# An attention-and-FFN layer on one core: a reordered prologue that issues from two queues

## Chip, core and metric

The kernel runs on one core of a Trainium2 chip. The metric is device time in microseconds, from one launch to its end; the median of three runs is compared.

## What is computed

Eight batches of 512 tokens with 128 channels pass an attention layer with 16 heads of 8 channels, a layer norm, a gated feed-forward layer and a second layer norm. The scores of a head are a sum of three things: a tanh of the scaled q.k product, a product of "soft bits" (hamming) and a "lattice" form of six features per token. The part that the change touches is the making of q, k and the features, and the constants behind them:

```python
qkv = (x @ qkv_w.T).reshape(b, t, 3, H, HD)
scores = sips_alpha[0] * jnp.tanh(raw / sips_beta[0])
soft_bits = jnp.tanh(x @ hex_w.T)
hamming = jnp.einsum('bid,bjd->bij', soft_bits, soft_bits) / 2.0
scores = scores + lam * hamming[:, None, :, :]
hexc = jnp.tanh(x @ q6_w.T)
w = jax.nn.softmax(transform_weights / TEMP, axis=-1)
Mh = jnp.einsum('ht,tde->hde', w, transforms)
lat = jnp.einsum('bid,hde,bje->bhij', hexc, Mh, hexc) / 6.0
attn = jax.nn.softmax(scores + lat * (jax.nn.sigmoid(scale_logit) * 2.0), axis=-1)   # causal
x = layernorm(x + out); r = sigmoid(xr @ W_r.T); k = relu(xk @ W_k.T) ** 2
x = layernorm(x + r * (k @ W_v.T))                                  # xr, xk mix x with the token before
```

## The kernel before, in words

Each batch has a period of 20 steps (`PAIRS`), numbered t. A step handles one "pair", a 128 x 1024 block of scores in one of three PSUM buffers (`raw`). For a pair TensorE makes q.k (`scores`), ScalarE takes the tanh (line 783), TensorE makes the bias (`biases`: lattice, hamming and a shift, one step later) in the same buffer, VectorE adds the two (`main`, line 1004), ScalarE takes the exponential three steps later (line 788), GpSimd masks it (line 892), and TensorE multiplies by v into `sums` (`weighted`). The buffer is free for pair t + 3 when `main` of pair t has run, so the engines go in a ring of three. Five pairs make a quad of four heads; quad 1 begins at t = 5.

q, k, J (the features as keys) and G (the features as queries, with the lattice matrices applied) are split into three bf16 levels each: `hi` is a rounding cast, `rest` the difference, `mid` a second cast, `lo` the last difference. They go to DRAM (`to_dram`) and come back replicated as stacks (`load_stack`), from which bf16 matmuls make the products at full precision. Everything in a batch's side work that passes through the one `side_bank` of PSUM is a "unit": xT (transposed x), q, k, F (features), G, v. Units have a fixed order; TensorE starts a unit when the reader of the one before has finished. A period makes units xT2, q2, k2, F2, G2 for two batches ahead and v1 for one batch ahead.

Engines execute in order, so the order in the code is the order of the work. Before the first period there is a prologue that is written out by hand:

- SyncE issues every load but those of x (line 352 on): x of batch 0, the q/k/v weights, the feature weights, then seven small constants (lines 359 to 363), the late weights (out_w, W_r, W_k, W_v, lines 366 to 370). `first_stacks` (line 447) then writes and loads q and k for the first four heads, J, G, the shift rows (line 465), heads 4 to 8, and heads 8 to 16, and writes the rows of batch 1.
- VectorE (line 1147 on) copies the weights, makes batch 0's q, k, J, G levels with GpSimd's help (`rest`, `lo`, lines 950 to 952), makes the lattice matrices, the bound that gives the shift (lines 1215 to 1226), the values of batch 0 (`values_in(0)`), then the late weights (lines 1231 to 1247), and then batch 1's units from `x_out(1)` on (line 1250).
- TensorE (line 689 on) runs units xT1, q1, k1, F1, the small lattice products, G1, v1, the scores of pair 0, then four late transposes (line 714), batch 1's xT2, q2, k2, F2, the scores of pair 1, G2, and enters period 0. There it runs batch 2's xT2 and then the bias of pair 0.

Of the kernel before, what the change touches and what calls it, by code (L numbers as in the profile page):

```python
# [25 lines left out]
ACT = mybir.ActivationFunctionType  # L26
# [6 lines left out]
DVE0_BETA = 6  # L33
DVE0_WEIGHTS = 10
DVE0_TWMAX = 12
# [4 lines left out]
DVE0_SHIFT = 30  # L40
DVE0_END = 37
# [31 lines left out]
ACT_UNITS = {"F1", "F2", "kk", "rr"}  # L73
FIRST_UNITS = ["xT1", "q1", "k1", "F1", "G1", "v1", "xT2", "q2", "k2", "F2", "G2"]
# [8 lines left out]
def period_uses(post, prep, values):  # L83

    return [use for t in range(PAIRS) for use in units_at(t, post, prep, values)]


class Side:
# [26 lines left out]
    def made(self, n, use):  # L115

        if use == "v" or isinstance(n, int) and n == 0:
            return self.through(n - 1, use + "1")
        return self.through(n - 2, use + "2")
# [20 lines left out]
def build(nc, x, qkv_w, out_w, hex_w, lam_logit, q6_w, transforms, transform_weights, scale_logit,  # L140
# [17 lines left out]
    with ExitStack() as ctx:  # L158
# [118 lines left out]
        x_in = sem("x_in")  # L277
# [7 lines left out]
        first_qk, first_g, second_in = sem("first_qk_in"), sem("first_g_in"), sem("second_in")  # L285
# [29 lines left out]
        def side_place(b, use):  # L315

            if use in ("q1", "k1"):
# [31 lines left out]

        @block.sync  # L350
        def _(sp):
# [24 lines left out]
            def to_dram(kind, par):  # L376

                done = scr_in[kind]
                if kind == Q:
                    sp.dma_start(q_rows[par].rearrange("l p i -> p l i"), parts[:, Q]).then_inc(done, 16)  # L380
                elif kind == K:

                    sp.dma_start(k_rows[par][0:LEVELS].rearrange("l p i -> p l i"), parts[:, K]).then_inc(done, 16)
                    sp.dma_start(k_rows[par][LEVELS:].rearrange("l p i -> p l i"),
                                 parts[:, K, 0:LEVELS - 1]).then_inc(done, 16)
                elif kind == J:
                    sp.dma_start(j_rows[par], parts[0:J_ROWS, J]).then_inc(done, 16)
                else:
# [971 lines left out]
```

## Time and profile before

| | us |
|---|---|
| median of three runs | 420.8 (420.11 to 423.27) |
| the profiled execution | 420.74 |
| its span, first to last instruction | 418.8 |
| busy: TensorE matmul, VectorE, ScalarE, GpSimd | 368.2, 332.7, 327.3, 230.6 |
| prologue: start of the first `main` | 47.53 |

The profile's busy shares are averages over the span: the prologue (the first 45 us) and the tail are sparse, the periods between them dense. What an instruction costs is read from its own row. The profiled execution's time is 1.9 us above its span.

### The profile page before, as it was taken

The page shows a single profiled execution, that of the slowest core. Times are in us where ns is not written, and L with a number is a line of the kernel's source. Part 1 is how long each engine was busy: PE and PEld are TensorE (multiplying, and loading weights), DVE is VectorE, ACT ScalarE, POOL GpSimd, SP SyncE. Part 2 cuts the span into 40 slices and gives each one's busy share as a digit, 9 for nine tenths or more (in the row PEclk, how much of TensorE's full clock was granted, in tenths as well). Part 3 has the DMA queues.
Part 4 walks back from the last instruction along what each step waited for, and adds up shares of the span by engine and source line. Part 5 has one row for each costly group of instructions (what it writes and reads, how often), then busy time and mean ns, then how long its engine had stood idle before and what let it go on. Part 6 is the DMA issues. An engine that isn't in the chain of part 4 may idle for free.

```text
span 418.8 us, 8760 instructions
## 1 busy us (share of the span) xinstructions
PE 368.2 (88%) x2907; PEld 191.3 (46%) x2907; DVE 332.7 (79%) x539; ACT 327.3 (78%) x364; POOL 230.6 (55%) x367
## 2 busy tenths in 40 slices
PE   4557798899999999999899989999989998999863
PEld 1232343345455544645364535454544554345442
DVE  4873677988988989798979897989887958786643
ACT  1002389999998989799889989899989998999621
POOL 4313535834687359644965488646873446344532
PEclk9999999999999999999999999999999999899978
DMA  3354587786621775167624764276318610100000
GB/s 100 94 144 121 162 275 189 232 236 166 200 84 48 205 193 172 49 164 195 190 80 121 188 182 131 85 194 186 123 52 206 173 59 7 45 27 1 2 27 25
DMA packets 37807, 53.74 MB, mean 128 GB/s; under 512 B 3522, under 2 KB 35266, under 8 KB 36190
## 3 DMA queue, kind: packets, MB, share of 16 engines
q1 hardware_dynamic: 34078, 51.49, 43.4%
q10 hardware_dynamic: 3696, 1.84, 1.8%
q8 instruction: 18, 0.29, 0.3%
q14 instruction: 15, 0.12, 0.1%
HBM read 38.69 MB, written 14.61 MB: 127 GB/s over the span
## 4 chain that ended last, share of the span: by engine, by line
PE 50%; DVE 15%; issue 10%; POOL 9%; SPq 7%; ACT 5%; DMA 3%; ACTq 1%; POOLq 0%; DVEq 0%
PE raw L511 22%; PE side_bank L511 13%; PE sums L511 12%; DVE probs L1004 6%; ACT probs L788 3%; PE side_bank L598 3%; POOL probs L892 2%; SPq L401 2%; ACT probs L783 2%; POOL x L927 2%; POOL x L923 2%; SPq L415 2%; POOL parts L905 2%; SPq L412 2%; DVE bn L1089 1%
## 5 line engine op out<-in xcount | busy, mean ns | idle before, releaser
L1004 DVE SCALAR_TENSOR_TENSOR probs<-probs,scal,raw 128x1024 f32<-128x1024 f32 x160 | 202.8, 1274 | 40.4 <-PE raw L511 39.4
L783 ACT ACTIVATE probs<-raw 128x1024 f32<-128x1024 f32 x160 | 163.9, 1025 | 33.2 <-PE raw L511 32.2
L892 POOL TENSOR_SCALAR_AFFINE_SELECT probs<-probs 128x256 f32<-128x256 f32 (+1 forms) x224 | 98.9, 458 | 131.6 <-ACT probs L788 131.1
L788 ACT ACTIVATE probs<-probs 128x1024 f32<-128x1024 f32 x160 | 169.3, 1060 | 0.9 <-DVE probs L1004 0.9
L511 PE MATMUL raw<-q_stack,k_stack 72*128 72x384 bf16 (+3 forms) x512 | 99.0, 306 | 10.9 <-DVE probs L1004 6.9
L511 PE MATMUL raw<-i_stack,j_stack 111*128 111x384 bf16 (+3 forms) x512 | 98.1, 304 | 2.7 <-ACT probs L783 2.5
L511 PE MATMUL sums<-probs,values 128*32 128x256 f32 (+2 forms) x1280 | 93.3, 391 | 5.1 <-POOL probs L892 4.1
L511 PEld LDWEIGHTS raw<-q_stack,k_stack 72*128 72x128 bf16 x512 | 38.9, 99 | 63.8 <-DVE probs L1004 35.3
L511 PEld LDWEIGHTS raw<-i_stack,j_stack 111*128 111x128 bf16 x512 | 42.4, 99 | 48.6 <-issue 15.3
L511 PEld LDWEIGHTS sums<-probs,values 128*32 128x32 f32 x1280 | 29.8, 109 | 50.9 <-issue 27.2
L899 POOL TENSOR_TENSOR whole<-whole,parts 128x512 f32<-128x512 f32 x22 | 26.2, 1189 | 23.1 <-DVE parts L1038 23.1
L905 POOL TENSOR_TENSOR parts<-whole,parts 128x512 bf16<-128x512 f32 x30 | 35.1, 1171 | 4.2 <-DVE parts L1043 4.2
L1043 DVE CAST parts<-whole 128x512 bf16<-128x512 f32 x32 | 19.6, 612 | 2.9 <-POOL whole L899 2.8
L915 POOL TENSOR_TENSOR rstd<-var_eps,minus_half 128x4 f32<-128x4 f32 x14 | 14.7, 1047 | 1.2
L796 ACT ACTIVATE feats<-side_bank 128x512 f32<-128x512 f32 x8 | 4.9, 611 | 12.4 <-PE side_bank L511 12.4
L511 PEld LDWEIGHTS side_bank<-w_r_mix,x1T 128*128 128x128 f32 x112 | 13.6, 191 | 1.0
L511 PE MATMUL side_bank<-w_r_mix,x1T 128*128 128x128 f32 x112 | 13.6, 275 | 0.0
L511 PE MATMUL side_bank<-x1T,w_k_mix 128*128 128x512 f32 x28 | 13.2, 591 | 0.0
L835 ACT ACTIVATE probs<-shift_col 1x1536 bf16<-1x1536 bf16 x1 | 1.5, 1481 | 14.6 <-DVE w_r_mix L1244 14.6
L1038 DVE CAST parts<-whole 128x512 bf16<-128x512 f32 x24 | 12.3, 511 | 0.7 <-DMA q_rows<-parts 0.5
L1089 DVE BATCH_NORM_STATS2 bn<-res 128x6 f32<-128x128 f32 x56 | 12.2, 280 | 0.2
L511 PE MATMUL side_bank<-xT,wqT 128*128 128x512 f32 x14 | 9.7, 781 | 2.9 <-DVE xT L1019 2.3
(144 smaller groups left out, 347.6 us busy)
## 6 DMA issues: line engine op xcount, KB each, us to landing
q_stack<-q_rows SPq DMA_DIRECT2D x21, 384.0 KB
k_stack<-k_rows SPq DMA_DIRECT2D x21, 384.0 KB
i_stack<-lattice_i SPq DMA_DIRECT2D x21, 288.0 KB
i_stack<-hamming_i SPq DMA_DIRECT2D x21, 288.0 KB
q_rows<-parts SPq DMA_DIRECT2D x8, 384.0 KB, 8.7
k_rows<-parts SPq DMA_DIRECT2D x8, 384.0 KB, 3.0
lattice_i<-parts SPq DMA_DIRECT2D x8, 288.0 KB
k_rows<-parts SPq DMA_DIRECT2D x8, 256.0 KB, 3.3
```

The costliest lines, as they stand in the source:

```text
L511: return nc.tensor.matmul(o, lhsT, rhs, start=start, stop=stop, **kw)
L598: last = nc.tensor.transpose(o[:, n * P:(n + 1) * P], src(n), ident[:])
L783: nc.scalar.activation(pair_probs(t), raw[:, t % PSUM_PAIRS, :].rearrange("p (u i) -> p u i", u=2), ACT.Tanh).then_inc(tanh_done, 1)
L788: nc.scalar.activation(pair_probs(t), pair_probs(t), ACT.Exp).then_inc(exp_done, 1)
L892: last = nc.gpsimd.affine_select(out=v, in_=v, compare_op=ALU.is_ge, fill=0.0, base=0, pattern=[[0, v.shape[1]], [1, P]], channel_multipli ...
L899: nc.gpsimd.tensor_tensor(whole[:, kind, :], feats[:] if kind == J else whole[:, kind, :], parts[:, kind, 0, :], ALU.subtract).then_inc(re ...
L905: nc.gpsimd.tensor_tensor(parts[:, kind, 2, :], whole[:, kind, :], parts[:, kind, 1, :], ALU.subtract).then_inc(lo_done[kind], 1)
L915: nc.gpsimd.tensor_tensor(rstd[:], var_eps[:], minus_half[:], ALU.pow).then_inc(rstd_done, 1)
L1004: v.scalar_tensor_tensor(out=o, in0=o, scalar=scal[:, 2:3], in1=raw[:, t % PSUM_PAIRS, :].rearrange("p (u i) -> p u i", u=2), op0=ALU.mult ...
L1038: v.tensor_copy(parts[:, kind, 0, :], feats[:] if kind == J else whole[:, kind, :]).then_inc(hi_done[kind], 1)
L1043: v.tensor_copy(parts[:, kind, 1, :], whole[:, kind, :]).then_inc(mid_done[kind], 1)
L1089: v.bn_stats(bn[:, blk, :], res[:, blk, :]).then_inc(bn_done, 1)
```

## The change

- The six loads of constants, tw and tr move from SyncE's queue to ScalarE's, at its very start. x of batch 1 is loaded into `x_res` by ScalarE (own semaphore) and no longer waits for `x_nat` to be free.
- Unit order: xT1, F1, q1, k0, G1, v1, xT2, q2, k2, F2, G2. Batch 0's k becomes a ScalarE unit, `k0`. ScalarE copies it and casts hi and mid; GpSimd makes rest and lo. GpSimd also makes J's levels first, where before k's came first.
- VectorE takes the maximum of tw and the feature weights first; the q and k weights come after. Its own q split stands behind the lattice map.
- ScalarE issues the loads of the J stack, the DRAM writes of G, the shift rows (ahead of the lattice rows) and the lattice rows of the first four heads. SyncE issues the hamming rows beside it.
- SyncE loads heads 4 to 16 in one piece (12 issues where there were 24). Quad 1 then waits for all of it.
- TensorE runs batch 1's xT2, q2, k2, F2 ahead of pair 0's scores. The late transposes go to period 0, step 3, into `sums`. VectorE's late weights and three of batch 1's `mid` casts go into period 0 (`FIRST`).

Core of the diff:

```diff
-ACT_UNITS = {"F1", "F2", "kk", "rr"}
-FIRST_UNITS = ["xT1", "q1", "k1", "F1", "G1", "v1", "xT2", "q2", "k2", "F2", "G2"]
+ACT_UNITS = {"k0", "F1", "F2", "kk", "rr"}
+FIRST_UNITS = ["xT1", "F1", "q1", "k0", "G1", "v1", "xT2", "q2", "k2", "F2", "G2"]
+LATE_WEIGHTS = 3
...
             def first_stacks():
-                for kind in (Q, K):
+                for kind in (J, Q, K):
                     sp.wait_ge(lo_done[kind], 1)
-                    to_dram(kind, 0)
+                    to_dram(sp, kind, 0)
                 for kind in (Q, K):
                     sp.wait_ge(scr_in[kind], 16 * SCR_DMAS[kind])
-                    load_stack(kind, 0, first_qk, (0, 4))
-                for kind in (J, G):
-                    sp.wait_ge(lo_done[kind], 1)
-                    to_dram(kind, 0)
-                sp.wait_ge(scr_in[J], 16 * SCR_DMAS[J])
-                load_stack(J, 0, stack_in[J])
+                    load_stack(sp, kind, 0, first_qk, (0, 4))
                 sp.wait_ge(scr_in[G], 16 * SCR_DMAS[G])
-                load_stack(G, 0, first_g, (0, 4))
-
-                sp.wait_ge(s_consts, 1)
-                for n in range(2):
-                    sp.dma_start(j_stack[n][SHIFT_ROW:BIAS_ROWS, :], shift_row).then_inc(s_const_rows, 16)
+                load_hamming(sp, 0, first_g, (0, 4))
                 for kind in (Q, K, G):
-                    load_stack(kind, 0, second_in, (4, 8))
-                for kind in (Q, K, G):
-                    load_stack(kind, 0, stack_in[kind], (8, H))
+                    load_stack(sp, kind, 0, stack_in[kind], (4, H))
                 write_rows(1, 1)
...
-            pe.wait_ge(s_dve0, DVE0_WEIGHTS)
-            for use in ("q1", "k1", "F1"):
-                side(-1, use)
+            pe.wait_ge(s_dve0, DVE0_FEATURES)
+            side(-1, "F1")
...
+            side(-1, "q1")
...
+            side(-1, "k0")
...
+            side(-1, "xT2")
+            side(-1, "q2")
+            side(-1, "k2")
+            side(-1, "F2")
             scores(0, 0, 0)
-            pe.wait_ge(s_w_late, 16 * 6)
-            pe.wait_ge(s_zero, 2)
-            transposed(raw[:, 2], [wo_perm] + [w_nat[:, n, :] for n in (4, 5, 6)]).then_inc(s_wT, 1)
-            for use in ("xT2", "q2", "k2", "F2"):
-                side(-1, use)
             scores(0, 0, 1)
             side(-1, "G2")
...
+            side(-1, "k0")
+            act.wait_ge(act_freed, side_units.through(-1, "k0"))
+            nc.scalar.activation(parts[:, K, 0, :], whole[:, K, :], ACT.Copy).then_inc(hi_done[K], 1)
+            act.wait_ge(rest_done[K], 1)
+            nc.scalar.activation(parts[:, K, 1, :], whole[:, K, :], ACT.Copy).then_inc(mid_done[K], 1)
+            act.wait_ge(scr_in[J], 16 * SCR_DMAS[J])
+            load_stack(act, J, 0, stack_in[J])
+            act.wait_ge(lo_done[G], 1)
+            to_dram(act, G, 0)
             act.wait_ge(s_dve0, DVE0_SHIFT)
             nc.scalar.activation(shift_row, shift_col[0:1].broadcast_to([1, LEVELS, T]),
                                  ACT.Copy).then_inc(s_consts, 1)
+            act.wait_ge(s_consts, 1)
+            for n in range(2):
+                act.dma_start(j_stack[n][SHIFT_ROW:BIAS_ROWS, :], shift_row).then_inc(s_const_rows, 16)
+            act.wait_ge(scr_in[G], 16 * SCR_DMAS[G])
+            load_lattice(act, 0, first_g, (0, 4))
...
-            for kind in (K, J):
+            for kind in (J, K):
                 rest(0, kind)
                 lo(0, kind)
...
+            FIRST = {0: [(mid, 1, K)], 1: [(mid, 1, J), (wo_heads,)], 3: [(mid, 1, G)], 4: [(late_weights,)]}
```

On TensorE, between unit v1 of batch 0 and the bias of pair 0 (`raw<-q_stack` is a pair's scores, `raw<-i_stack` a pair's bias, `raw<-ident,probs` the late transposes), before:

```order
L511 MATMUL side_bank<-wvT,xT0 128x128 x4
L511 MATMUL raw<-q_stack0,k_stack0 128x512 x2
L685 MATMUL raw<-ident,probs 128x128 x4
L598 MATMUL side_bank<-ident,x_nat 128x128 x4
L511 MATMUL side_bank<-xT1,wqT 128x512
L511 MATMUL side_bank<-xT1,wkT 128x512
L511 MATMUL side_bank<-xT1,w_fT 128x512
L511 MATMUL raw<-q_stack0,k_stack0 128x512 x2
L511 MATMUL side_bank<-feats,lat_map 128x512
L598 MATMUL side_bank<-ident,x_nat 128x128 x4
L511 MATMUL raw<-i_stack0,j_stack0 128x512 x2
```

and after:

```order
L514 MATMUL side_bank<-wvT,xT0 128x128 x4
L604 MATMUL side_bank<-ident,x_res 128x128 x4
L514 MATMUL side_bank<-xT1,wqT 128x512
L514 MATMUL side_bank<-xT1,wkT 128x512
L514 MATMUL side_bank<-xT1,w_fT 128x512
L514 MATMUL raw<-q_stack0,k_stack0 128x512 x4
L514 MATMUL side_bank<-feats,lat_map 128x512
L604 MATMUL side_bank<-ident,x_nat 128x128 x4
L514 MATMUL raw<-i_stack0,j_stack0 128x512 x2
```

The late transposes are gone from here, and both pairs' scores stand behind batch 1's F2. No unit was removed between v1 and the first bias.

On VectorE, from the last of the shift values to the first `main` (the SCALAR_TENSOR_TENSOR row), before:

```order
L1055 COPY values0<-side_bank 128x8x4x8 x2
L1236 COPY probs<-probs 128x4x8 x4
L1238 TENSOR_SCALAR mu_prev<-mu 128x2
L1240 COPY woT<-raw 128x128
L1243 TENSOR_SCALAR w_r_mix0<-raw,mu 128x128
...
L1246 TENSOR_SCALAR w_vT<-raw 128x128
L1019 COPY xT1<-side_bank 128x512
...
L1038 CAST parts<-whole 128x512
L1043 CAST parts<-whole 128x512 x2
L1019 COPY xT0<-side_bank 128x512
L1004 SCALAR_TENSOR_TENSOR probs<-probs,scal,raw 128x1024 x2
```

and after, on to the fifth `main`:

```order
L1100 COPY values0<-side_bank 128x8x4x8 x2
L1064 COPY xT1<-side_bank 128x512
...
L1064 COPY xT0<-side_bank 128x512
L1088 CAST parts<-whole 128x512
L1049 SCALAR_TENSOR_TENSOR probs<-probs,scal,raw 128x1024
L1088 CAST parts<-whole 128x512
L1201 COPY probs<-probs 128x4x8 x4
...
L1049 SCALAR_TENSOR_TENSOR probs<-probs,scal,raw 128x1024
L1208 COPY woT<-sums 128x128
...
L1214 TENSOR_SCALAR w_vT<-sums 128x128
L1049 SCALAR_TENSOR_TENSOR probs<-probs,scal,raw 128x1024
```

The late weights stood ahead of the copy of batch 1's xT; now they stand between the fourth and the fifth `main`, and the casts and head copies between the first and the second.

## Rows read from the trace of the kernel before

**Rows 1.** Page, chain that ended last, shares of the span by engine
```profile
PE 50%; DVE 15%; issue 10%; POOL 9%; SPq 7%; ACT 5%; DMA 3%; ACTq 1%; POOLq 0%; DVEq 0%
```
**Rows 2.** Stretches: busy us by engine, granted clock, DMA share, GB/s
```profile
0.00:45.00 45.00, 26.52 (x64) 11.33 (x65) 27.08 (x71) 6.38 (x9) 16.45 (x22) 1.00 0.39 113
28.00:42.00 14.00, 9.95 (x18) 3.88 (x18) 6.13 (x15) 3.26 (x4) 4.18 (x4) 1.00 0.36 108
54.70:60.00 5.30, 5.01 (x31) 1.97 (x29) 4.52 (x5) 4.85 (x6) 1.18 (x3) 1.00 1.00 330
100.00:150.00 50.00, 48.29 (x414) 26.05 (x413) 43.82 (x68) 45.24 (x51) 32.16 (x50) 1.00 0.49 139
```
**Rows 3.** Timeline of TensorE: start us, us, instruction, idle before and releaser
```profile
19.14 2.07 PE L511 MATMUL side_bank<-feats,lat_map 128*128 128x512 f32 x2 [1.18 <-DVE lat_map L1198]
32.36 2.05 PE L511 MATMUL side_bank<-xT,wqT 128*128 128x512 f32 x2 [2.29 <-DVE xT L1019]
40.96 2.04 PE L511 MATMUL side_bank<-feats,lat_map 128*128 128x512 f32 x2
44.77 1.06 PE L511 MATMUL raw<-i_stack,j_stack 111*128 111x512 bf16 x2
45.62 1.06 PE L511 MATMUL raw<-q_stack,k_stack 72*128 72x384 bf16 x4
48.85 1.03 PE L511 MATMUL raw<-q_stack,k_stack 72*128 72x384 bf16 x4 [1.32 <-DVE probs L1004]
54.79 0.60 PE L511 MATMUL raw<-i_stack,j_stack 111*128 111x384 bf16 x4
110.19 1.02 PE L511 MATMUL side_bank<-feats,lat_map 128*128 128x512 f32 x2
```
**Rows 4.** Timeline of VectorE, prologue and period 0
```profile
21.32 0.69 DVE L1062 COPY whole<-side_bank 128x512 f32<-128x512 f32 x1 [1.01 <-PE side_bank L511]
26.89 0.76 DVE L1055 COPY values<-side_bank 128x256 f32<-128x256 f32 x2
29.32 0.29 DVE L1240 COPY woT<-raw 128x128 f32<-128x128 f32 x1 [1.26 <-PE raw L685]
31.52 0.69 DVE L1019 COPY xT<-side_bank 128x512 f32<-128x512 f32 x1
44.18 0.42 DVE L1043 CAST parts<-whole 128x512 bf16<-128x512 f32 x1
45.64 1.36 DVE L1043 CAST parts<-whole 128x512 bf16<-128x512 f32 x1 [1.04 <-POOL whole L899]
47.53 2.46 DVE L1004 SCALAR_TENSOR_TENSOR probs<-probs,scal,raw 128x1024 f32<-128x1024 f32 x2
58.55 0.49 DVE L1038 CAST parts<-whole 128x512 bf16<-128x512 f32 x1 [0.49 <-DMA q_rows<-parts]
58.96 2.46 DVE L1004 SCALAR_TENSOR_TENSOR probs<-probs,scal,raw 128x1024 f32<-128x1024 f32 x2
```
**Rows 5.** Timeline of ScalarE
```profile
15.35 0.60 ACT L796 ACTIVATE feats<-side_bank 128x512 f32<-128x512 f32 x1 [4.23 <-PE side_bank L511]
40.71 1.93 ACT L783 ACTIVATE probs<-raw 128x1024 f32<-128x1024 f32 x2
```
**Rows 6.** Timeline of GpSimd
```profile
17.43 1.15 POOL L905 TENSOR_TENSOR parts<-whole,parts 128x512 bf16<-128x512 f32 x1 [1.01 <-DVE parts L1043]
```
**Rows 7.** The chain in order of time: transfers, from issue to landing
```profile
6.41 3.87 DMA tr_sb<-in_L_attn_transforms
53.51 4.95 DMA q_rows<-parts
```
**Rows 8.** Timeline of SyncE's queue: the time an issue holds it
```profile
5.93 0.43 SPq L362 DMA_DIRECT2D tw<-L_attn_transform_weights  x1
28.67 0.75 SPq L412 DMA_DIRECT2D i_stack<-lattice_i  x1
33.49 1.48 SPq L465 DMA_DIRECT2D j_stack<-probs  x2
```

More of the change, by code:

```diff
@@ new lines, in load_stack @@
+        def load_stack(eng, kind, par, ready, heads=(0, H)):
+            first, n = heads[0] * T, (heads[1] - heads[0]) * T
+            if kind in (Q, K):
+                for copy in range(LEVELS):
+                    levels = q_rows[par] if kind == Q else k_rows[par][copy:copy + LEVELS]
+                    src = levels.rearrange("l (d h) i -> (l d) (h i)", h=H)
+                    eng.dma_start((q_stack if kind == Q else k_stack)[par][copy:QK_ROWS:LEVELS, first:first + n],
+                                 src[:, first:first + n]).then_inc(ready, 16)
+            if kind == J:
+                for at, row in ((0, 0), (LAT_ROWS, HEX_J)):
+                    eng.dma_start(j_stack[par][at:at + LAT_ROWS, :],
+                                 j_rows[par][row:row + LEVELS * NB].rearrange("p l i -> (p l) i")
+                                 ).then_inc(ready, 16)
+            if kind == G:
+                load_lattice(eng, par, ready, heads)
+                load_hamming(eng, par, ready, heads)
@@ new lines, in load_lattice, with load_hamming @@
+        def load_lattice(eng, par, ready, heads):
+            first, n = heads[0] * T, (heads[1] - heads[0]) * T
+            for copy in range(LEVELS):
+                eng.dma_start(i_stack[par][copy:LAT_ROWS:LEVELS, first:first + n],
+                              lattice_i[par].rearrange("l (e h) i -> (l e) (h i)", h=H)[:, first:first + n]
+                              ).then_inc(ready, 16)
+        def load_hamming(eng, par, ready, heads):
+            first, n = heads[0] * T, (heads[1] - heads[0]) * T
+            for copy in range(LEVELS):
+                eng.dma_start(i_stack[par][LAT_ROWS + copy:SHIFT_ROW:LEVELS, first:first + n]
+                              .rearrange("e (h i) -> e h i", i=T),
+                              hamming_i[par].rearrange("l e i -> (l e) i").unsqueeze(1)
+                              .broadcast_to([LEVELS * NB, n // T, T])).then_inc(ready, 16)
@@ L676, in period @@
                         side(b, use)
+                    if not post and t == LATE_WEIGHTS:
+                        late_weights()
                     if post:
@@ L1129, in period @@
                         stage(b + 2, *a)
+                    for stage, *a in FIRST.get(t, []) if not post else []:
+                        stage(*a)
                     if values and t in VALUES_UNITS:
@@ L1190, in _ @@
             mark(DVE0_TW)
-            mid(0, K)
             dve.wait_ge(s_twT, 1)
@@ L1200, in _ @@
             mark(DVE0_LATTICE)
+            rest_here(Q)
+            mid(0, J)
+            mid(0, Q)
+            lo_here(Q)
             link(v.tensor_reduce(lat_abs[:], lat_map[0:NB, 0:NB * H].rearrange("d (e h) -> d h e", h=H), AX.X,
@@ L1210, in _ @@
             hi(0, G)
-            mid(0, J)
             rest_here(G)
```

205 lines of the change are left out of this document (97 added, 108 removed).

## The prediction

> **What bounds the kernel now.** I read the chain of waits first. TensorE holds half of it and no transfer more than a few per cent [rows 1]. The stretches then say where: from 100 us on TensorE is busy 48.3 of 50 us, and that work is the same after the change. The first 45 us have 26.5 us of TensorE work, 27.1 of VectorE and 6.4 of ScalarE [rows 2]: nobody is full there, so a chain of single steps sets the pace. The change touches only this part and period 0. The question is how much earlier the first `main` starts than at 47.53 us [rows 4], and how much of that is left once the ring of three buffers runs.
>
> Following the timelines back from 47.53: VectorE had to make batch 1's `mid` of G (45.64, 1.36 us) and copy xT2 first. The bias of pair 0 started at 44.77 on TensorE behind G2 (40.96), and this behind F2, k2 and q2 (32.36). q2 waited 2.29 us for the copy of xT, which ran at 31.52, behind the late weights on VectorE [rows 3, 4]. Pair 0's tanh at 40.71 stood behind F2's tanh in ScalarE's order [rows 5], not behind its data. The loads are off this path: the last shift row was issued by 34.97 [rows 8], ten microseconds before the bias used it.
>
> **The change, part by part.**
>
> *Start of the prologue.* The small constants gate VectorE. Before, the last of them, tr, was SyncE's eleventh issue, at 6.41, and landed 3.87 us later [rows 7]. On ScalarE's queue it is the sixth issue at about 0.46 us each [rows 8], so it leaves at 3.1 and lands at 7.0 (5.9 if a landing takes 2.8). I take 6.8. From there I replay with durations of rows: two small reductions and the feature weights to 7.5, F1 on TensorE 2.1 us to 9.6, its tanh 0.60 [rows 5] to 10.3, q1 to 12.5, q copied to 13.3, k0 to 15.4, k0's copy on ScalarE to 16.0. G1 waits for that copy, since it shares the bank order, and starts at 16.1; before it started at 19.14 [rows 3]. The ScalarE copy and casts of k are not in the trace: by the 0.60 of a tanh of the same shape from PSUM, and the 1.93 us of two blocks of twice the size [rows 5], they cost 0.5 to 1.0; I take 0.60. VectorE meanwhile does J, q's four steps and the lattice work until about 18.5, and so reads G1 at 18.5 where it did at 21.32 [rows 4]. From that read to the end of `values_in(0)` it took 6.3 us (21.32 to 27.6). The same work follows; one 0.4 us cast has left it and a GpSimd subtraction may stand against a cast (0.42 became 1.36 [rows 4]). So `values_in(0)` ends at 24.5, range 23.8 to 25.4.
>
> *Late weights out of the prologue.* Before, from the end of `values_in(0)` at 27.6 to the copy of xT at 31.52 lay head copies, a wait of 1.26 us for the late transposes and six copies of weights [rows 4]. After, xT2 starts on TensorE as soon as the bank is read: 24.5 + 1.1 = 25.6 for the copy. The copy is 5.9 us earlier. x of batch 1 has been in `x_res` since before 10 us, so nothing waits for it.
>
> *From that copy to the first main.* Before: 47.53 - 31.52 = 16.0 us. The units are the same. Pair 0's scores are added in front of G2: +0.85 (two 512-column matmuls at the rate of the prologue, start to start 44.77 to 45.62 [rows 3]). `mid` of J and `mid` of G, with their 0.42, 1.04 of waiting and 1.36 [rows 4], leave, and one `mid` (K, 0.43) comes: xT2's transposes then end last instead, and the net is -1.4. So 15.4 us, and the first `main` is at 41.0: 6.5 us earlier.
>
> *Loads.* k's levels: J takes GpSimd to 16.2, then rest, ScalarE's mid and lo (1.15 each on GpSimd [rows 6]) put k's last level at 20.0, 1.4 later than before. The six q and k loads end their issues at about 25.3 and land near 27.5. Pair 0's scores now stand behind F2, at 34.1, so 6 us of cover hide it. ScalarE issues two J loads, two G writes, two shift rows (1.48 [rows 8]) and three lattice loads, some 0.7 us each, and is free at 29; F2 asks for it at 34.3. If the cover went, each late microsecond would count once. Heads 4 to 16: 3.1 MB in 12 issues from 27.6. At the 330 GB/s of a full queue [rows 2] this lands by 38; pair 5 needs it near 50. Cost nothing.
>
> What queues do is weighed here. The rows show that a second issuer saves issue time: an issue holds a queue 0.43 to 0.75 us [rows 8], while DMA ran at 0.36 of its capacity from 28 to 42 us [rows 2]. The Trainium skill, page DMA: Bandwidth & Descriptors, section "Issuing engines are not separate DMA queues", says that transfers from ScalarE and SyncE share the same 16 engines and that a second issuer saves sequencer time only. By that rule the sum stays as it is, since I credited the second queue with issue time alone; a reader who hoped for doubled bandwidth would be told no.
>
> *What period 0 gives back.* Between the first `main` and the sixth lay 58.96 - 47.53 = 11.4 us [rows 4]. VectorE now has there five mains (1.23 each, 2.46 for two [rows 4]) 6.2, casts of J and G 0.85, head copies 0.6, q and k copies 1.45, late weights 2.2 (29.32 to 31.52 [rows 4]) and q's hi 0.45: 11.8, and with the gaps between them 12.4. That is 1.0 us more than before even if TensorE never limits: the lower bound of this term. TensorE runs the prologue at its lower level: G takes 2.04 at 40.96 and 1.02 at 110.19, and the bias of pair 3 at 54.79 is the first at 0.60 where 1.06 was usual [rows 3]. That is 1.2 GHz and then 2.4 GHz, although the granted clock reads 1.00 throughout [rows 2]; ahead of the rise TensorE had worked without a gap from 48.85 [rows 3]. If it rises no sooner in relation to the pairs, the late transposes add 0.9 us of TensorE before bias 3, and the late weights (2.2 us) then stand fully between main 3 and main 4: 2.7 in all, the upper bound. The stretch F2, two scores, G2 (32.2 to 37.9) is now longer by one pair's scores, and the rise may come there or at the biases. I take 1.4, nearer the lower end, because the gap ahead of pair 3's scores is filled sooner.
>
> *Back on the other side.* Rows of batch 1 were issued at 53.51 and landed 4.95 later [rows 7], and VectorE sat 0.49 us on them ahead of a cast at 58.55 [rows 4], with period 0 waiting for DMA here and there. SyncE reaches those rows at about 37 to 47 now. I credit 0.6, that wait and little more, range 0 to 1.1.
>
> Sum: 6.5 - 1.4 + 0.6 = 5.7 us. All is read from the profiled execution of 420.74 us (span 418.8), which lies within 0.1 of the median 420.8. 420.74 - 5.7 = 415.0.
>
> **Rivals.**
>
> *The rise comes before G2.* Then pair 1's scores, G2 and the transposes take half: 0.4 + 1.0 + 0.5, the first main at 39.0, and 8.5 - 1.0 + 0.6 = 8.1 us: 412.6. For: the dense stretch is one pair's scores longer. Against: G2 ran at the lower level to its end at 43.0, with F2 and pair 1's scores close ahead of it [rows 3]. The Trainium skill, page TensorE: Matmul & The Clock Gate, Part 1, holds that sustained work lifts the engine from half rate; by it this case is the likelier one, and the row at 45.62 (still 1.06 after 1.8 us of work) neither proves nor refutes it.
>
> *The late weights stand fully in the ring.* TensorE stays at 1.2 GHz until pair 3, 2.7 us are given back and little of the DMA credit arrives: 6.5 - 2.7 + 0.2 = 4.0: 416.8. For: six linked instructions that nothing overlaps on VectorE, with `main` of pair 4 behind them and pair 7's scores behind that.
>
> *The lead is lost.* If batch 0's chain is no faster (constants late, GpSimd against VectorE), 3 us go, and with 2.7 given back the result is near 420. Against: each link has its row.
>
> *The other side: quad 1 waits for heads 4 to 16.* One mechanism: TensorE's wait at pair 5 for 3.1 MB that was 1 MB before. At 330 GB/s it lands by 38. At the 108 GB/s of 28 to 42 us [rows 2] it lands at 56.5, where pair 5's bias stood before: from that rate down the kernel is no faster, and at 92 GB/s, 61.5, it is 4 us slower: 425. Against: the 108 were limited by issues of 72 KB; these are four times as large.
>
> **How the numbers follow.** Forecast 415.0, its own range 413.5 to 416.5: 0.45. Early rise, 412.6: 0.2. Late weights in the ring, 416.8: 0.23. Lead lost, 420: 0.08. Quad 1 waits, 425: 0.04. A measurement of this kernel tells about 1% (4.2 us) from no change, so faster means under 416.6. The forecast counts there nearly whole, the early rise whole, the late-weights case a third: 0.72. Within 1%: 0.25; slower: 0.03. The range of 8 in 10 goes from 411.8 to 418.4.
>
> **What would show it.** Right: G1 at 16 to 17; the copy of batch 1's xT at 24.5 to 26.5 with no late weights ahead; first `main` at 40 to 42; sixth `main` 12.4 to 14.1 after the first; periods 1 to 7 of unchanged length. Wrong: a first `main` after 43, an idle row of TensorE that a stack load ends at pair 5, a ScalarE issue that holds F2's tanh, or a period 0 more than 3 us longer than before.

## The result and the profile after

In 20 runs of each, side by side, the changed kernel took 417.19 us (median, 414.46 to 421.57) and the kernel before 422.7 us (418.96 to 424.79). The ratio is 0.9875, with a 95% interval of 0.9849 to 0.9902; here and in the table below, ratios leave out the slow executions, more than 1.5% above the fastest of their kernel (three of the changed kernel's 20, and the profiled one of e2 among others). The prediction's own ratio was 415.0 / 420.74 = 0.9864, inside that interval. The absolute median is 2.2 us above the forecast; the kernel before itself had a median 1.9 us higher in these 20 runs than in the three shown first. The profiled execution of the changed kernel took 417.11 us with a span of 415.4, so the profiled spans differ by 3.4 us where the medians differ by 5.5.

The chain that ended last, page of the changed kernel (against [rows 1]):

```profile
PE 54%; DVE 14%; issue 10%; POOL 10%; ACT 7%; DMA 1%; SPq 1%; ACTq 1%; POOLq 0%; DVEq 0%
```

SyncE's queue had 7% of the chain and DMA 3%; now each has 1%. What left the chain is SyncE's issuing and the landing of transfers; what grew is TensorE (50% to 54%) and ScalarE (5% to 7%). The stretches of the changed kernel, columns as in [rows 2]:

```profile
0.00:45.00 45.00, 29.13 (x73) 12.24 (x74) 25.53 (x61) 9.85 (x14) 16.31 (x23) 1.00 0.52 144
36.00:40.00 4.00, 3.41 (x6) 0.98 (x4) 1.25 (x3) 2.53 (x3) 2.27 (x2) 1.00 0.75 184
40.00:44.00 4.00, 3.74 (x13) 2.02 (x14) 3.22 (x7) 0.88 (x1) 1.48 (x2) 1.00 0.62 163
44.00:48.00 4.00, 2.15 (x13) 1.09 (x12) 3.96 (x7) 2.11 (x3) 2.12 (x2) 1.00 0.80 229
100.00:150.00 50.00, 48.28 (x416) 25.97 (x415) 44.86 (x67) 45.39 (x51) 30.92 (x49) 1.00 0.52 143
```

The last row is the old one: the steady part did not change. The first 45 us hold 2.6 us more of TensorE's work than before. The middle rows are stretches in which heads 4 to 16 load, beside batch 1's row writes: 163 to 229 GB/s for everything that moved, not the 330 of [rows 2].

TensorE's timeline, changed kernel (against [rows 3]):

```profile
4.83 1.09 PE L604 MATMUL side_bank<-ident,x_nat 128*128 128x128 f32 x4 [4.83 <-DMA x_nat<-in_L_attn_x]
7.99 1.09 PE L695 MATMUL raw<-ident,probs 128*128 128x128 f32 x4 [2.07 <-DMA probs<-in_L_attn_hex_w]
9.53 2.08 PE L514 MATMUL side_bank<-xT,w_fT 128*128 128x512 f32 x2 [0.45 <-DVE w_fT L1234]
18.02 2.05 PE L514 MATMUL side_bank<-feats,lat_map 128*128 128x512 f32 x2 [0.73 <-issue]
37.49 1.91 PE L514 MATMUL side_bank<-feats,lat_map 128*128 128x512 f32 x2
41.17 1.06 PE L514 MATMUL raw<-i_stack,j_stack 111*128 111x512 bf16 x2
45.24 0.60 PE L514 MATMUL raw<-i_stack,j_stack 111*128 111x384 bf16 x4
53.00 0.60 PE L514 MATMUL raw<-i_stack,j_stack 111*128 111x512 bf16 x2 [0.48 <-DMA i_stack<-hamming_i]
```

In the kernel before, the weights' transposes were at

```profile
5.16 1.09 PE L685 MATMUL raw<-ident,probs 128*128 128x128 f32 x4 [0.35 <-DMA probs<-in_L_attn_hex_w]
```

Now they wait for the feature weights (`hex_w`) until 7.99, 2.8 us later; F1 can't start before 9.53 (the prediction had 7.5), and G1 follows at 18.02 (16.1). The bias of pair 0 stands at 41.17, 3.6 us earlier than before. It still runs at the lower of the two rates (1.06); the first at 0.60 is pair 2's at 45.24, where it was pair 3's at 54.79. The row at 53.00 is pair 5's bias, and a load ends its idle time: one of the prediction's signs of being wrong, here with 0.48 us. That idle time did not delay the sixth `main`: VectorE's timeline has no idle row from 42.02 to it.

VectorE's, changed kernel (against [rows 4]):

```profile
7.51 0.15 DVE L1229 TENSOR_REDUCE tw_sum<-tw 16x1 f32<-16x7 f32 x1 [0.79 <-DMA tr_sb<-in_L_attn_transforms]
9.19 0.29 DVE L1234 COPY w_fT<-raw 128x128 f32<-128x128 f32 x1 [1.35 <-PE raw L695]
20.17 0.69 DVE L1107 COPY whole<-side_bank 128x512 f32<-128x512 f32 x1 [0.15 <-PE side_bank L514]
27.33 0.69 DVE L1064 COPY xT<-side_bank 128x512 f32<-128x512 f32 x1 [1.21 <-PE side_bank L604]
42.35 1.28 DVE L1049 SCALAR_TENSOR_TENSOR probs<-probs,scal,raw 128x1024 f32<-128x1024 f32 x1
43.88 2.37 DVE L1201 COPY probs<-probs 128x32 f32<-128x32 f32 x4
46.35 1.28 DVE L1049 SCALAR_TENSOR_TENSOR probs<-probs,scal,raw 128x1024 f32<-128x1024 f32 x1
53.84 1.28 DVE L1049 SCALAR_TENSOR_TENSOR probs<-probs,scal,raw 128x1024 f32<-128x1024 f32 x1
55.37 2.46 DVE L1049 SCALAR_TENSOR_TENSOR probs<-probs,scal,raw 128x1024 f32<-128x1024 f32 x2
```

tr was waited for until 7.51, where 6.8 was said, and the weights came last of all. First `main` 42.35 (5.2 us earlier than before), second 46.35, sixth 55.37 (3.6 earlier). At the start of period 1 the lead is 3.6 (84.84 against 88.48), at the last `main` 3.5 (389.4 against 392.9), in the span 3.4. Almost nothing is won or lost in seven periods.

The landing times at the start, DMA issues in 0 to 9 us of the changed kernel, KB each and median us from issue to landing:

```profile
x_nat<-in_L_attn_x SPq DMA_DIRECT2D x1, 256.0 KB, 3.9
probs<-in_L_attn_qkv_w SPq DMA_DIRECT2D x1, 192.0 KB, 5.1
scal<-in_L_attn_sips_beta ACTq DMA_DIRECT2D x1, 0.5 KB, 3.1
```

and of the kernel before:

```profile
x_nat<-in_L_attn_x SPq DMA_DIRECT2D x1, 256.0 KB, 2.8
probs<-in_L_attn_qkv_w SPq DMA_DIRECT2D x1, 192.0 KB, 2.9
scal<-in_L_attn_sips_beta SPq DMA_DIRECT2D x1, 0.5 KB, 2.8
```

x lands 1.1 us later and the q/k/v weights 2.2 us later, now that the constants (four of them 0.5 KB each, spread over 128 partitions) leave from the second queue from 0.80 on, and batch 1's x (256 KB) at 3.80.

SyncE's queue, changed kernel (against [rows 8]):

```profile
37.53 2.33 SPq L408 DMA_DIRECT2D i_stack<-hamming_i  x3
39.90 4.07 SPq L363 DMA_DIRECT2D q_rows<-parts  x1
44.64 4.18 SPq L367 DMA_DIRECT2D k_rows<-parts  x1
59.52 2.18 SPq L400 DMA_DIRECT2D i_stack<-lattice_i  x3
61.75 10.43 SPq L408 DMA_DIRECT2D i_stack<-hamming_i  x3
```

The last load of batch 0 is issued by 39.9, and TensorE gets it at 53.0: 13 us later. Heads 4 to 16 are 3.1 MB, issued from 30.79 on, so they came at 140 GB/s. Behind them single issues hold the queue for 4 us, and three hamming loads of batch 1 for 10.4, where the three of batch 0 took 2.33. I read this as issues that stand behind data that has not moved yet; no run isolates it.

### The profile page after: what moved, and what is told of

Its sections match the earlier page's. It is cut to its first block, busy times and chain, and to the rows that moved or that the text cites. A ratio compares the mean times of both kernels' runs of the same rounds, so it can differ in the third digit from the quotient of the medians.

```text
span 415.4 us, 8750 instructions
## 1 busy us (share of the span) xinstructions
PE 365.9 (88%) x2907; PEld 190.6 (46%) x2907; DVE 331.3 (80%) x536; ACT 329.3 (79%) x367; POOL 229.8 (55%) x367
## 4 chain that ended last, share of the span: by engine, by line
PE 54%; DVE 14%; issue 10%; POOL 10%; ACT 7%; DMA 1%; SPq 1%; ACTq 1%; POOLq 0%; DVEq 0%
PE raw L514 23%; PE side_bank L514 16%; PE sums L514 11%; DVE probs L1049 6%; ACT probs L810 4%; PE side_bank L604 3%; ACT probs L805 3%; POOL probs L937 2%; POOL x L972 2%; POOL x L968 2%; POOL parts L950 2%; DVE bn L1134 1%; DMA probs<-in_L_attn_hex_w 1%; DVE whole L1072 1%; POOL whole L944 1%
## 5 line engine op out<-in xcount | busy, mean ns | idle before, releaser
L1049 DVE SCALAR_TENSOR_TENSOR probs<-probs,scal,raw 128x1024 f32<-128x1024 f32 x160 | 203.0, 1274 | 40.7 <-PE raw L514 37.7
L944 POOL TENSOR_TENSOR whole<-whole,parts 128x512 f32<-128x512 f32 x22 | 25.8, 1172 | 12.0 <-DVE parts L1083 11.5
L1088 DVE CAST parts<-whole 128x512 bf16<-128x512 f32 x31 | 17.3, 562 | 1.8 <-POOL whole L944 1.7
L944 POOL TENSOR_TENSOR whole<-feats,parts 128x512 f32<-128x512 f32 x8 | 9.5, 1189 | 7.4 <-DVE parts L1083 7.4
L1083 DVE CAST parts<-whole 128x512 bf16<-128x512 f32 x23 | 12.4, 539 | 0.2
L1112 DVE COPY sums_sb<-sums 128x512 f32<-128x512 f32 x15 | 10.3, 686 | 2.0 <-PE sums L514 2.0
```

Source lines behind the costliest of these rows:

```text
L944: nc.gpsimd.tensor_tensor(whole[:, kind, :], feats[:] if kind == J else whole[:, kind, :], parts[:, kind, 0, :], ALU.subtract).then_inc(re ...
L1049: v.scalar_tensor_tensor(out=o, in0=o, scalar=scal[:, 2:3], in1=raw[:, t % PSUM_PAIRS, :].rearrange("p (u i) -> p u i", u=2), op0=ALU.mult ...
L1083: v.tensor_copy(parts[:, kind, 0, :], feats[:] if kind == J else whole[:, kind, :]).then_inc(hi_done[kind], 1)
L1088: v.tensor_copy(parts[:, kind, 1, :], whole[:, kind, :]).then_inc(mid_done[kind], 1)
```

## Experiments

Every kernel ran five rounds beside the kernel before, in three groups: e1 to e4 (median of the kernel before 421.39), e5 to e8 (421.88) and e9 to e11 (421.23). Between groups only ratios compare. The marks are starts in each one's profile, in us. "Sixth" is sixth `main` minus first; "period 1" is the start of period 1's first `main`.

| run | median us (range) | ratio, 95% | first `main` | sixth | period 1 |
|---|---|---|---|---|---|
| before (first profile) | 422.7 | 1 | 47.53 | 11.4 | 88.5 |
| changed (first profile) | 417.19 | 0.9875 [0.9849, 0.9902] | 42.35 | 13.0 | 84.8 |
| e1 changed, again | 416.55 (415.05 to 417.36) | 0.9897 [0.9858, 0.9937] | 41.47 | 13.0 | 83.9 |
| e2 late work in gaps | 417.25 (414.43 to 420.77) | 0.9900 [0.9864, 0.9936] | 39.14 | 15.4 | 87.0 |
| e3 constants on SyncE | 417.45 (415.34 to 417.68) | 0.9906 [0.9875, 0.9937] | 41.16 | 13.0 | 85.2 |
| e4 before + late part | 423.45 (421.56 to 425.82) | 1.0060 [1.0028, 1.0091] | 44.97 | 13.9 | 91.5 |
| e5 loads in two pieces | 417.66 (416.08 to 421.26) | 0.9914 [0.9886, 0.9941] | 41.23 | 13.8 | 84.6 |
| e6 = e2 + e5 | 418.98 (417.39 to 421.59) | 0.9935 [0.9909, 0.9962] | 41.42 | 8.5 | 85.1 |
| e7 = e6, constants behind x | 418.15 (416.11 to 421.32) | 0.9931 [0.9900, 0.9962] | 41.49 | 8.5 | 83.9 |
| e8 = e6 + filler | 417.61 (416.22 to 422.18) | 0.9933 [0.9899, 0.9967] | 38.63 | 8.5 | 84.7 |
| e9 loads in turn | 417.67 (414.69 to 421.34) | 0.9913 [0.9878, 0.9948] | 41.10 | 14.0 | 84.5 |
| e10 = e8 + e9 | 417.75 (415.86 to 418.89) | 0.9916 [0.9883, 0.9949] | 40.72 | 8.5 | 84.6 |
| e11 = e7 + e10 | 417.39 (415.53 to 419.9) | 0.9917 [0.9890, 0.9945] | 40.61 | 8.5 | 82.7 |

**e1: the changed kernel again**, beside e2 to e4.

> The changed kernel once more, as the yardstick of this chip. First theory (two terms ate the missing lead: weights that land late, and late work in period 0): weights' transposes near 8.0 us, first main 42.0 to 42.8, sixth main 13.0 us after the first, ratio to before 0.985 to 0.991. Rival (the moment at which TensorE goes to full rate decides, and moves from run to run): first main as before but the distance to the sixth main differs by over 1 us from 13.0.

Same code, first `main` 0.9 earlier. TensorE's timeline of e1 says why:

```profile
37.46 1.52 PE L514 MATMUL side_bank<-feats,lat_map 128*128 128x512 f32 x2
39.83 0.66 PE L604 MATMUL side_bank<-ident,x_nat 128*128 128x128 f32 x4 [0.85 <-DVE whole L1107]
40.32 0.60 PE L514 MATMUL raw<-i_stack,j_stack 111*128 111x512 bf16 x2
```

G2 starts at 37.46 in e1 and 37.49 in the first profile, but takes 1.52 instead of 1.91, and bias 0 takes 0.60 instead of 1.06. The rise to 2.4 GHz came inside G2 here (the trace's granted clock rises at 38.5) and after pair 1's bias there (44.0). So 1 us of lead hangs on when the same program is granted its rate, and one profile's marks are good to about a microsecond; e2 against e6 will show 2.3. The distance to the sixth `main` is 13.0 in both, so the rival of this run falls.

**e2: the late work in idle stretches of the prologue.**

```diff
-            FIRST = {0: [(mid, 1, K)], 1: [(mid, 1, J), (wo_heads,)], 3: [(mid, 1, G)], 4: [(late_weights,)]}
+            FIRST = {0: [(mid, 1, K)], 1: [(mid, 1, J)], 3: [(mid, 1, G)]}
...
             values_in(0)
+            wo_heads()
             x_out(1)
+            late_weights()
```

(and TensorE's late transposes behind batch 1's xT2.)

> Head copies after values_in(0), late transposes behind batch 1's xT2, late weights behind its copy: all in idle stretches of VectorE (1.21 and 2.23 us) and TensorE (0.87 us). First theory: first main 42.4 to 43.0, sixth main 10.5 to 11.5 us after it instead of 13.0, so 1.5 to 2.3 us under the changed kernel. Rival (late work is hidden in period 0 anyway, TensorE's rate decides): sixth main again about 13 us after the first, time within 0.5 us of the changed kernel.

The profiled execution took 420.77, the longest of e2's eight, so it is read for where the waits are. First `main` 39.14 and the fifth at 46.1, 6.8 us earlier than in e1; then TensorE's timeline of e2 has

```profile
53.24 1.03 PE L514 MATMUL raw<-i_stack,j_stack 111*128 111x512 bf16 x2 [6.37 <-DMA i_stack<-hamming_i]
```

and VectorE's

```profile
54.23 0.43 DVE L1082 CAST parts<-whole 128x512 bf16<-128x512 f32 x1 [6.83 <-DMA q_rows<-parts]
```

Pair 5's bias starts at 53.24, as it did at 53.00 with the late work in the ring, and batch 1's q rows, written behind the same loads, hold VectorE just as long. The sixth `main` follows the first by 15.4 us, where 10.5 to 11.5 was expected: the 7 us are all paid back in these waits, and from 50.9 to 61.1 TensorE is at the lower rate:

```profile
50.90:61.10 10.20, 7.86 (x40) 3.97 (x44) 3.65 (x5) 3.83 (x4) 2.20 (x3) 0.50 0.77 220
```

So with the late work out of the ring, SyncE's transfers and not VectorE set pair 5. In the ring that work costs little, since the transfers are not ready much sooner.

The early first `main` is not the edit's. e6 has the same prologue, and its first `main` is at 41.42, as in e1. The k2 unit in TensorE's timeline of e2, and in that of e6:

```profile
31.20 1.13 PE L514 MATMUL side_bank<-xT,wkT 128*128 128x512 f32 x2 [0.91 <-DVE whole L1071]
31.23 2.07 PE L519 MATMUL side_bank<-xT,wkT 128*128 128x512 f32 x2 [0.91 <-DVE whole L1078]
```

e2's granted clock rose at 30.4, that of e6 at 38.2. The 2.3 us between them are TensorE's rate.

**e3: the constants back on SyncE**, behind the feature weights, with VectorE's weights first. This undoes the queue part of the change.

```diff
-            act.dma_start(scal[:, 3:4], beta.partition_broadcast(P)).then_inc(s_beta, 16)
+            sp.dma_start(scal[:, 3:4], beta.partition_broadcast(P)).then_inc(s_beta, 16)
...
+            act.wait_ge(x_in, 16)
             act.dma_start(x_res[:], x[1]
```

> The six constant loads go back to SyncE behind the feature weights, VectorE copies the weights ahead of the maximum of tw, x of batch 1 waits for x of batch 0. First theory (4-byte packets on the second queue delay x and the weights): x lands at 3.7 and the weights' transposes start at 5.2 instead of 8.0; tr lands at 10 to 10.5, so the lattice map comes no earlier; first main 41.5 to 43.0, time within 1 us of the changed kernel. Rival (early constants are what made the prologue faster): first main at 44 or later, time 2 us above.

VectorE's timeline of e3:

```profile
5.13 0.69 DVE L1065 COPY xT<-side_bank 128x512 f32<-128x512 f32 x1 [1.30 <-PE side_bank L609]
6.41 0.29 DVE L1230 COPY w_fT<-raw 128x128 f32<-128x128 f32 x1 [0.58 <-PE raw L700]
9.93 0.15 DVE L1239 TENSOR_REDUCE tw_sum<-tw 16x1 f32<-16x7 f32 x1 [2.26 <-DMA tr_sb<-in_L_attn_transforms]
```

w_fT is copied at 6.41 instead of 9.19, so x and weights come early when the constants and batch 1's x leave the start. Both were taken away together, so their shares are not separated. Then tr comes at 9.93 instead of 7.51, TensorE has its transpose of tw ahead of q1 and waits 2.77 us for it, and q1 starts at 11.7 (12.3 in e1), G1 at 17.4 (18.0). The two orders come out within 0.6 us at G1, 0.3 at the first `main`, and alike in the time. The second queue for the constants earned nothing that these runs can tell; the gain is elsewhere.

**e4: the kernel before, with only the late weights moved** into period 0 (head copies step 1, transposes step 3, weights step 4).

> The kernel before with one part alone: late transposes, head copies and late weights moved to steps 1, 3 and 4 of period 0. First theory: first main 2.8 to 3.6 us earlier (43.9 to 44.7), 1.5 to 2.5 of it given back by the sixth main, time 0.8 to 2 us under before. Rival (nothing is given back): 3 to 3.6 us under before.

The first `main` came 2.6 us earlier (2.8 to 3.6 was expected), and the kernel was slower: 1.006, where 0.8 to 2 us of gain was expected. VectorE's timeline of e4:

```profile
58.57 0.43 DVE L1047 CAST parts<-whole 128x512 bf16<-128x512 f32 x1 [1.76 <-DMA q_rows<-parts]
58.91 1.27 DVE L1013 SCALAR_TENSOR_TENSOR probs<-probs,scal,raw 128x1024 f32<-128x1024 f32 x1
```

The same cast waited 0.49 for q_rows in the kernel before and ran at 58.55 [rows 4]. SyncE issued those rows at 53.89 (53.51 before [rows 7]) behind its 24 loads, whatever the engines did. The sixth `main` was pinned to that: 58.91, against 58.96 before. From there to period 1 e4 loses 3.1 us more (32.6 us against 29.5), and in that stretch lies the second of two with TensorE at the lower rate:

```profile
46.30:49.70 3.40, 3.40 (x10) 1.51 (x11) 2.15 (x7) 1.97 (x2) 0.20 (x1) 0.50 0.70 210
60.00:66.80 6.80, 6.56 (x36) 3.78 (x37) 2.55 (x5) 1.97 (x2) 1.24 (x3) 0.50 0.76 204
```

Each begins around the end of a wait of TensorE for a buffer that VectorE's `main` frees, the first for the first `main`, the second for the sixth, the one that q_rows held up:

```profile
46.30 1.04 PE L511 MATMUL raw<-q_stack,k_stack 72*128 72x384 bf16 x4 [3.32 <-DVE probs L1013]
60.24 1.03 PE L511 MATMUL raw<-q_stack,k_stack 72*128 72x384 bf16 x4 [2.33 <-DVE probs L1013]
```

So this shorter chain was worth nothing without SyncE's shorter list. The reverse, SyncE's list alone, was not run.

**e5: heads 4 to 8 and 8 to 16 loaded apart**, q rows of batch 1 written between them, otherwise as changed.

```diff
                 for kind in (Q, K, G):
-                    load_stack(sp, kind, 0, stack_in[kind], (4, H))
-                write_rows(1, 1)
+                    load_stack(sp, kind, 0, second_in, (4, 8))
+                sp.wait_ge(lo_done[Q], 2)
+                to_dram(sp, Q, 1)
+                for kind in (Q, K, G):
+                    load_stack(sp, kind, 0, stack_in[kind], (8, H))
+                write_rows(1, 1, (K, J, G))
```

> The changed kernel with one edit: heads 4 to 16 come in two pieces again (4 to 8, then 8 to 16), with batch 1's q rows written between them. First theory, as it stands after four runs (in the changed kernel the loads of heads 4 to 16 and batch 1's row writes land just when period 0 asks for them, and VectorE's late work sets the pace): the 0.48 us wait of pair 5's bias on the hamming load goes, first main 41.5 to 42.5, sixth main 12.4 to 13.0 us after it, time within 1 us of the changed kernel. Rival (the loads already set the pace): sixth main under 11.5 us after the first, time 2 us lower.

No wait for a load is left at pair 5, the sixth `main` is at 55.1 (54.5 in e1), and the ratio is e1's within the intervals: with the late work in the ring, VectorE is at pair 5 when the load is. The two limits coincide there. The distance to the sixth `main` is 13.8, not the 12.4 to 13.0 expected; TensorE was at half rate from 48.2 to 51.6 in this profile.

**e6: e2 and e5 together**, which takes both away.

> Late work in the prologue's idle stretches, as in the run before, and the two-piece loads with early q rows. First theory: the 6.4 us wait of pair 5's bias and VectorE's 6.8 us wait on batch 1's q rows go, sixth main 10 to 11 us after the first at 39 to 41.5, time 2 to 4 us under the changed kernel. Rival (the loss came from TensorE's rate, which fell there, and not from the transfer): a stall of over 3 us between the fifth and the sixth main stays.

The sixth `main` now follows the first by 8.5 us instead of 13.0. That 4.5 is what the late work and the transfers behind it cost in period 0. The seventh `main` is at 51.2 against 55.7 in e1. But the time is 418.98, where 2 to 4 us under the changed kernel was expected. TensorE's timeline of e6, at the start of batch 1's stack:

```profile
78.35 0.66 PE L611 MATMUL side_bank<-ident,x_nat 128*128 128x128 f32 x4 [1.32 <-DMA x_nat<-in_L_attn_x]
83.99 1.03 PE L519 MATMUL raw<-i_stack,j_stack 111*128 111x512 bf16 x2 [3.44 <-DMA i_stack<-hamming_i]
```

and its stretches around it:

```profile
72.00:82.50 10.50, 7.05 (x72) 3.10 (x72) 5.64 (x6) 8.55 (x10) 4.26 (x7) 1.00 0.76 207
82.50:92.70 10.20, 8.71 (x28) 4.71 (x29) 5.28 (x6) 4.51 (x6) 1.81 (x4) 0.50 0.79 229
```

Period 1's first bias waits for batch 1's hamming rows until 83.99. The lead is gone there, and TensorE is at half rate for 10.2 us from 82.5 on: period 1 took 47.4 us where 44.4 is usual. SyncE began to issue batch 1's stack at 53.4 here and at 53.95 in the changed kernel: it had not come earlier with the engines. The split puts 24 issues ahead of it instead of 12.

**e7: e6, and the constants on ScalarE's queue only after x landed, VectorE's weights first.**

> As e6, and the constants are issued by ScalarE only when x of batch 0 has landed, VectorE copying the weights first. First theory: x lands at 3.7 instead of 4.8, the weights' transposes start before 6 instead of 8.0, first main 0.5 to 1.5 us ahead of e6 at the same rate of TensorE. Rival (weights that land late are hidden by other steps): first main as in e6.

Batch 1's xT2 starts at 26.00 (26.21 in e6) and the first `main` is at 41.49 (41.42), as the rival said: the earlier weights show nowhere. Period 1's bias waits 3.34 us for hamming rows, to 82.82. The same wall.

**e8: e6, and two matmuls more** (identity by ones, f32, into `sums`, never read) behind v1, to raise TensorE's rate sooner. They are added work.

> As e6, with two products of the identity with ones (fp32, 512 columns, into the unused sums bank) in TensorE's idle stretch behind v1; they are extra work that nothing reads. If TensorE's rate in the prologue is set by how busy it is, it rises before 30 us and q2, k2, F2 and G2 take 1.1 us instead of 2.05: first main at 37.5 to 39. If the rate rises at a moment of its own, units stay at 2.05 and the first main is 0.3 to 0.6 later than in e6.

The first `main` is at 38.63, 2.8 earlier than in e6, the seventh at 48.4, with the granted clock rising at 26.5. It rose at 24.2 and 24.0 in e10 and e11, which have the same filler, and at 30.4, 38.2 and 38.5 in e2, e6 and e7 without it. But in e10 and e11 it fell again near 31 for 6.9 us, and their first `main` is at 40.7 and 40.6, while e2 had 39.14 without filler. So in these six profiles the rise comes earlier with the filler; that the first `main` does is not shown. Then TensorE's timeline of e8:

```profile
83.65 1.03 PE L519 MATMUL raw<-i_stack,j_stack 111*128 111x512 bf16 x2 [6.77 <-DMA i_stack<-hamming_i]
```

7 us of lead over e1 at the seventh `main`, and a wait of 6.77 to nearly the same time as in e6.

**e9: lattice and hamming loads issued in turn** instead of three and three, otherwise as changed.

```diff
-                load_lattice(eng, par, ready, heads)
-                load_hamming(eng, par, ready, heads)
+                for copy in range(LEVELS):
+                    load_lattice(eng, par, ready, heads, (copy,))
+                    load_hamming(eng, par, ready, heads, (copy,))
```

> The changed kernel, with the lattice and hamming loads of a stack issued in turn again, as before, instead of three and three (the last of the three hamming issues held SyncE for most of 10.4 us there). First theory (in the changed kernel no load of batch 1's stack is waited for, so their order shows nowhere yet): SyncE gets through batch 1's stack in 14 to 16 us instead of 18.2, periods and time as in the changed kernel within 1 us. Rival (the grouped order costs time in every period): 1.5 us or more lower.

**e10: e8 and e9 together.**

> As e8, with the two kinds of loads in turn. Theory now: period 0 ended 3 to 5 us early in e6 to e8 but batch 1's first bias waited 3.3 to 6.8 us for its hamming loads, landing near 83 to 84, and TensorE's rate fell in that wait. If the grouped order makes them late, they land by 81, the wait shrinks to under 3 us, and the time is 2 to 4 us under e8's 417.6. If it is the amount of data between 22 and 84 us, they land at 83 to 84 again and the time stays within 1 us of e8.

e9 came as its first theory said, with no wait at period 1. SyncE's issues of batch 1's whole stack took 14.2 us in it (52.40 to 66.6) where the changed kernel took 18.2 (53.95 to 72.2), but 17.9 in e10. In e10 period 1's bias waited 5.20 us for hamming rows, to 83.51, as e8's did to 83.65, and the time is within 0.2 us of e8's. There the order of issue did not change when the last rows arrive.

**e11: all edits together.** A candidate to beat the changed kernel.

> All edits together: late work in idle stretches, two-piece loads, two filling products, constants behind x, loads in turn. First theory: as e10 with the first main 0.2 to 1 us earlier, and the same arrival of batch 1's stack, so a time within 0.5 us of e10. Rival (a shorter prologue still counts): 1 us or more under e10.

417.39, ratio 0.9917 against e1's 0.9897, within each other's intervals. Its wait at period 1, TensorE's timeline of e11:

```profile
81.83 0.87 PE L520 MATMUL raw<-i_stack,j_stack 111*128 111x512 bf16 x2 [3.63 <-DMA i_stack<-hamming_i]
```

Nothing that was run beats the changed kernel.

## Why the prediction was right, point by point

The sign and the mechanism held: a shorter chain brings the first `main` forward, a part is given back in period 0, and the rest stays to the end. The ratio held too. But against the first profile (lead at the first `main` 5.2, at the sixth 3.6, in the span 3.4) and e1 (6.1, 4.5, and 5.5 in the span of 413.3), the forecast of 6.5, 5.1 and 5.7 lies above both.

In the forecast's own terms the first profile gives 5.2 - 1.6 + 0.05 = 3.6 us where 6.5 - 1.4 + 0.6 = 5.7 stood, and e1 gives 4.5, with 0.8 more of its 5.5 won in the tail, which the forecast left alone. That the medians lie 5.5 us apart, near 5.7, is in part luck: the terms do not add up to it. The fastest of the 20 runs of each lie 4.5 apart. Of the signs named, the distance to the sixth `main` (13.0) and the unchanged periods came as said; G1 (18.02), the copy of batch 1's xT (27.33) and the first `main` (42.35, in e1 41.47) came late, and one sign of being wrong appeared, the idle row at pair 5.

*Start of the prologue: 1.9 us too early.* The constants came 0.7 late (tr at 7.51, said 6.8). The step "feature weights to 7.5" failed by more: F1 started at 9.53, behind weights whose transposes waited for their load until 7.99. The working moved the constants to another queue and kept the old landing of x and weights. From F1 to G1 the replay gave 8.6 us and the trace has 8.5; to the end of `values_in(0)` the miss stayed at 1.6. It was said of this step that each link has its row; the landing in the new company had none. The Trainium skill, page DMA: Bandwidth & Descriptors, section "Issuing engines are not separate DMA queues", has both queues share the same 16 engines. It was used in the prediction to refuse a gain. The trace agrees and shows a loss besides: +1.1 us for x, +2.2 for the q/k/v weights, +2.8 for the feature weights. e3 shows that the loads moved to the second queue's start account for it (6.41 instead of 9.19), and that putting them back as a whole returns only 0.3 to the first `main`, since tr is then late.

*Late weights out of the prologue.* Right. 26.1 to 27.33, that is 1.2 us from the values to the copy of xT where 1.1 was said.

*From that copy to the first main.* 15.0 measured, 15.4 said; 14.2 in e1, whose rate rose inside G2. The rival "rise before G2" came half true in e1: the bias of pair 0 at 0.60, the first `main` at 41.47, not 39.0. It had priced pair 1's scores, G2 and the transposes at the full rate; the scores and part of G2 (1.52 us) were done before the rise. e2, where the clock rose at 30.4, had its first `main` at 39.14.

*Loads cost nothing.* True in the sum, wrong in the working. "Lands by 38" was 53.0. The rate of 330 GB/s came from a stretch of [rows 2] at full DMA share; these 3.1 MB came at 140, while all that moved was 163 to 229 with shares of 0.62 to 0.80, and they were issued from 30.79, not 27.6. The other-side rival (at 108 GB/s they land at 56.5) had the right place and the nearer rate: had the load come 4 us later, it would have been that case, and e2 shows it by bringing the engines forward instead (6.37 us of waiting). In the changed kernel the price was 0.48 us of idle TensorE and nothing at the sixth `main`. That it cost nothing is in part luck: VectorE, with the late weights and head copies that took 2.37 us, got there no sooner than the load.

*What period 0 gives back.* 1.6 in the first profile and in e1 (13.0 against 11.4), said 1.4 with bounds 1.0 to 2.7. Right in size, though part of its makeup differs: the head copies took 2.37 us instead of the 0.43 of before, in parallel with GpSimd's work, and so the second `main` came 4.0 us after the first. e6 bounds the whole cost of late work and load together at 4.5 us.

*Back on the other side.* 0.6 was credited for SyncE's earlier rows. In the first profile and in e1 the lead grows by 0.05 from the sixth `main` to period 1, and what the rows gave before the sixth is not seen apart from the rest. But e4 shows that the term was conceived too small and in the wrong place: without it the lead over the first five pairs is worth nothing, since the rows pinned the sixth `main` at 58.9. It was no credit on top but a condition of the whole gain.

*The rivals.* "Lead lost" fell: each chain step shortened. "Late weights fully in the ring" (416.8) is near the measured 417.19 in number, but by another sum: the give-back was 1.6, not 2.7, and it was the prologue that lacked 1.3 in the first profile.

*What stays open.* Why the stack loads run at a DMA share of 0.6 to 0.8 with the queue full, and so whether batch 1's arrival at 82 to 84 us could move: neither the order of issue (e10) nor the time at which period 0 runs (e6, e8, e11) moved it by more than 2.2 us. But SyncE began to issue that stack at 51.8 to 54.2 in the changed kernel and in every run made from it (58.7 before), so none of these runs tests an earlier start. Fewer bytes, or fewer descriptors, were not tried. Also open is how much of the medians' 5.5 us comes from the rate: the clock rose at 54.7 in the profile before and at 44.0 in the changed one, all these kernels spread over 2 to 7 us from run to run, and their profiles differ in where TensorE has half-rate stretches.

## What to carry to other kernels

When a prologue chain is shortened, ask where its lead will be spent: walk the next two or three arrivals (here q rows, then quad 1, then the next batch's stack) and write down when each lands whatever the engines do; the lead ends at the first of them that does not move too. A move of small loads to a second queue is to be costed with the landing of its new neighbours, not only its own. And time a load by a stretch in which loads of the same kind ran, not by the fullest stretch of the trace.

## What the runs showed of the hardware

- Four small copies of 32 columns on VectorE (`probs<-probs`, f32, strided) took 0.43 us together before and in e6 (26.08), and 2.37 in period 0 of the changed kernel, with GpSimd busy at 43.63 (1.35) and 44.94 (1.18). In e4 they stand in period 0 too, at 46.16, after GpSimd's work ended at 45.68, and took 0.42. That GpSimd is the cause fits all four but was not isolated.
- TensorE's rate fell during or right after idle stretches: in e2 in a wait for a load of 6.37 us, in e6 in one of 3.44, in e8 in one of 6.77, and in e4 at the end of two waits for VectorE of 3.3 and 2.3 us. The half rate then lasted 3.4 to 10.2 us. What this costs on top of the wait varies: period 1, behind the wait for batch 1's rows, took 47.4 us in e6, and 45.1 to 46.1 in e7, e8, e10 and e11, where 44.4 is usual. The Trainium skill, page TensorE: Matmul & The Clock Gate, Part 1, says that sustained work lifts the rate; the three kernels with filler (e8, e10, e11) agree (rise at 24.0 to 26.5, against 30.4 to 38.5 in e2, e6 and e7), and e1 against the first profile (38.5 and 44.0) shows that the same program gets it at different times.
- A queue's issues can be held for long: 10.43 us for three hamming loads of batch 1, where batch 0's took 2.33, with everything behind them waiting too.
